# Cross-attention of a decoder: keys placed by DMA, scores from high and low parts, another order of the loop

## What is computed

```python
def _L0_xattn_ref(q, k, v, Wq, bq, Wk, bk, Wv, bv, Wo, bo):
    HEADS, D_MODEL = 16, 256
    D_K = D_MODEL // HEADS
    qh = (q @ Wq + bq).reshape(B, LQ, HEADS, D_K).transpose(0, 2, 1, 3)
    kh = (k @ Wk + bk).reshape(B, LKV, HEADS, D_K).transpose(0, 2, 1, 3)
    vh = (v @ Wv + bv).reshape(B, LKV, HEADS, D_K).transpose(0, 2, 1, 3)
    scores = jnp.einsum('bhqd,bhkd->bhqk', qh, kh) * (1.0 / np.sqrt(D_K))
    out = jnp.einsum('bhqk,bhkd->bhqd', jax.nn.softmax(scores, axis=-1), vh)
    return out.transpose(0, 2, 1, 3).reshape(B, LQ, D_MODEL) @ Wo + bo

x = x + _L0_attn_ref(_layernorm(x), ...)
x = x + _L0_xattn_ref(_layernorm(x), ctx_512, ctx_512, ...)
x = x + _L0_ffn_ref(_layernorm(x), ...)
```

## Time and profile before

| | us |
|---|---|
| median of 3 runs | 3157.49 (3156.26 to 3159.41) |
| the profiled execution | 3159.65 |
| its span, from the first instruction to the last | 3158.1 |
| of it PE busy | 2933.1 (93%) |
| DVE busy | 2325.5 (74%) |
| ACT busy | 1862.7 (59%) |
| POOL busy | 921.5 (29%) |

### The profile page before, as it was taken

How to read it: one execution, slowest core, us unless ns; L and a number is a source line. 1 busy time by engine, 2 the same in 40 slices (tenths; PEclk the granted TensorE clock), 3 DMA queues, 4 the chain that set the end, 5 groups by cost and what they waited for, 6 DMA issues and landing times. The chain is left out here.

```text
span 3158.1 us, 35422 instructions
## 1 busy us (share of the span) xinstructions
PE 2933.1 (93%) x11342; PEld 1989.8 (63%) x11343; DVE 2325.5 (74%) x3334; ACT 1862.7 (59%) x2796; POOL 921.5 (29%) x590
## 2 busy tenths in 40 slices
PE   4799999999999999999999999999999977997995
PEld 3566666666666665666566656665666635775563
DVE  7778888888887888887878788879787826763111
ACT  3666676667666776777677767776777713441121
POOL 5004231423152315231513151315131133333002
PEclk8899999999999999999999999999999987996998
DMA  5001101110111001100110011001100008000012
GB/s 129 1 1 23 26 8 32 27 27 6 30 27 27 12 25 27 27 17 19 26 27 17 19 26 27 17 19 26 28 17 4 1 3 269 0 0 24 12 45 77
DMA packets 210193, 92.90 MB, mean 29 GB/s; under 512 B 147056, under 2 KB 203632, under 8 KB 210000
## 3 DMA queue, kind: packets, MB, share of 16 engines
q1 hardware_dynamic: 207360, 83.30, 10.2%
q0 software_dynamic: 2640, 7.21, 0.7%
HBM read 80.24 MB, written 10.22 MB: 29 GB/s over the span
## 5 line engine op out<-in xcount | busy, mean ns | idle before, releaser
L341 PE MATMUL PS<-XTHI,WHI 128*128 128x512 f32 x1536 | 655.5, 427 | 60.8 <-DVE EX L641 41.5
L342 PE MATMUL PS<-XTLO,WHI 128*128 128x512 f32 x1536 | 614.1, 400 | 0.0
L343 PE MATMUL PS<-XTHI,WLO 128*128 128x512 f32 x1536 | 613.6, 399 | 0.0
L269 POOL TENSOR_TENSOR RSTD<-MV,EPS 128x4 f32<-128x4 f32 x68 | 41.1, 605 | 1537.7 <-DVE MV L713 1529.8
L391 PE MATMUL Y<-H,W2S 128*128 128x512 f32 x1024 | 458.2, 596 | 2.7 <-DVE R L703 2.7
L391 PE MATMUL Y<-ATT,WO 128*128 128x512 f32 x1024 | 451.7, 594 | 4.1 <-ACT ATT L540 2.7
L540 ACT ACTIVATE ATT<-INV,CC,CE 128x128 f32<-128x128 f32 x1024 | 424.9, 481 | 3.7 <-DVE INV L687 3.7
L341 PEld LDWEIGHTS PS<-XTHI,WHI 128*128 128x128 f32 x1536 | 294.5, 192 | 153.6 <-issue 64.6
L505 ACT ACTIVATE EX<-PS,BNEG 128x512 f32<-128x512 f32 x256 | 169.8, 686 | 309.9 <-PE PS L343 307.6
L342 PEld LDWEIGHTS PS<-XTLO,WHI 128*128 128x128 f32 x1536 | 294.8, 192 | 83.6 <-issue 20.3
L343 PEld LDWEIGHTS PS<-XTHI,WLO 128*128 128x128 f32 x1536 | 294.0, 191 | 70.0
(11 more groups left out here) (180 smaller groups left out, 4823.9 us busy)
## 6 DMA issues: line engine op xcount, KB each, us to landing
STAGE<-L_attn_Wk SPq DMA_DIRECT2D x128, 64.0 KB, 2.1
STAGE<-L_attn_Wv SPq DMA_DIRECT2D x128, 64.0 KB, 2.1
STAGE<-L_attn_Wq SPq DMA_DIRECT2D x128, 64.0 KB, 2.1
WO<-L_attn_Wo SPq DMA_DIRECT2D x8, 1024.0 KB, 5.5
W2S<-L_attn_W SPq DMA_DIRECT2D x8, 1024.0 KB, 5.6
STAGE<-L_attn_W SPq DMA_DIRECT2D x64, 128.0 KB, 3.7
WGU<-L_ffn_r_gate SPq DMA_DIRECT2D x8, 512.0 KB, 10.2
WGU<-L_ffn_r_up SPq DMA_DIRECT2D x8, 512.0 KB, 9.5
```

Of the source, the lines that this page charges most:

```text
L341: nc.tensor.matmul(out, whi[:, kc, :], xhi[:, kc, :], start=(kc == 0), stop=False)
L342: nc.tensor.matmul(out, whi[:, kc, :], xlo[:, kc, :], start=False, stop=False)
L343: ins = nc.tensor.matmul(out, wlo[:, kc, :], xhi[:, kc, :], start=False, stop=(kc == KD - 1))
```

## The change

The host hands the context over transposed, and it is loaded per sequence straight into CT; CTXS, CSEQ, their copies and one transpose go. ScalarE writes the keys and the queries as high parts (KT[:, 0], QHI) in the type float32r; a new step `residues` on VectorE computes their low parts from the same PSUM bank (KT[:, 1], QLO). KX is filled with zeros once, by GpSimd, and `apart` is now on SyncE: eight DMAs for each half and sequence, each of which copies both parts of the keys of one head, 16 partitions by 2 by 128, to that head's columns. MASK and the mask product go. `scores` sums three float32r products in place of one float32 product. KT has one buffer: `qk(b+1)` waits until the DMAs of sequence b have landed. The loads for the experts move from SyncE's queue to GpSimd's. And the order changes: on TensorE make_qk(b+1) goes to the head of the iteration, and scores(b+1, 0) behind project(b-1) and turn_inputs(b+2); on ScalarE qk(b+1) goes ahead of turned_weights(b, 0); on VectorE residues(b+1) stands ahead of shifted(b, 1).

```diff
-        QT = sb("XQT", [P, 2, KD, P])
-        KT = sb("XKT", [P, 2, KD, P])
-        KX = sb("XKX", [P, 2, CH, SEQ])
+        QHI = sb("XQHI", [P, 2, KD, P], F32R)
+        QLO = sb("XQLO", [P, 2, KD, P], F32R)
+        KT = sb("XKT", [P, 2, KD, P], F32R)
+        KX = sb("XKX", [P, KD, 2, CH, SEQ], F32R)
...
+            def apart(i, j, c):
+                b = 2 * i + j
+                sp.wait_ge(k_lo, b + 1)
+                if not (type(i) is int and b == 0):
+                    sp.wait_ge(s_mm, b * KD + c - 1)
+                for h in range(CH):
+                    rows = slice(h * XK, (h + 1) * XK)
+                    sp.dma_start(KX[rows, c, :, h, :].bitcast(F32), KT[rows, :, c, :].bitcast(F32)).then_inc(kx[c], 16)
...
-                sp.dma_start(CTXS[:, bs, :], ctx_in[bs, :, :].rearrange("b s d -> s b d")).then_inc(x_in[k], 16)
+            def load_ctx(i, j):
+                b = 2 * i + j
+                if not (type(i) is int and i == 0):
+                    sp.wait_ge(v_mm, b - 1)
+                sp.dma_start(CT[:, j, :], ctx_in[bass.ds(b, 1), :, :].rearrange("b d s -> d (b s)")).then_inc(ct_in[j], 16)
...
+            sp.wait_ge(kx_zero, 1)
+            def sequence(i, j, more):
+                for c in range(KD):
+                    apart(i, j, c)
+                if more:
+                    load_ctx(i + 1, j)
...
+            nc.gpsimd.memset(KX[:, :, :, :, :].bitcast(F32), 0.0).then_inc(kx_zero, 1)
...
-            def apart(i, j, c):
-                u = (2 * i + j) * KD + c
-                pool.wait_ge(kt, 2 * i + (j + 1))
-                if not (type(i) is int and u < 2):
-                    pool.wait_ge(s_mm, u - 1)
-                nc.gpsimd.tensor_tensor(KX[:, c, :, :], bcast(KT[:, j, c, :], CH), MASK[:, :, :], ALU.mult).then_inc(kx, 1)
...
-                nc.tensor.transpose(A[:, 2 * P:3 * P], CSEQ[:, j, :], ident[:, :]).then_inc(zct_mm, 1)
...
+            def make_qk(b, j, i):
+                pe.wait_ge(ct_in[j], 16 * i + 16)
                 pe.wait_ge(zct, b + 1)
...
             def make_v(b, j):
-                pe.wait_ge(qt, b + 1)
-                pe.wait_ge(kt, b + 1)
+                pe.wait_ge(q_lo, b + 1)
...
             def scores(b, j, c):
                 u = b * KD + c
-                pe.wait_ge(kx, u + 1)
+                pe.wait_ge(kx[c], (b + 1) * 16 * CH)
+                pe.wait_ge(q_lo, b + 1)
                 if not (type(b) is int and u < 2):
                     pe.wait_ge(sh, u - 1)
                 for hf in range(2):
-                    ins = nc.tensor.matmul(S[:, c, hf * 512:(hf + 1) * 512], QT[:, j, c, :],
-                                           KX[:, c, hf * 4:(hf + 1) * 4, :].rearrange("p h s -> p (h s)"),
-                                           start=True, stop=True)
+                    out = S[:, c, hf * 512:(hf + 1) * 512]
+                    hi, lo = (KX[:, c, part, hf * 4:(hf + 1) * 4, :].rearrange("p h s -> p (h s)") for part in range(2))
+                    nc.tensor.matmul(out, QHI[:, j, c, :], hi, start=True, stop=False)
+                    nc.tensor.matmul(out, QHI[:, j, c, :], lo, start=False, stop=False)
+                    ins = nc.tensor.matmul(out, QLO[:, j, c, :], hi, start=False, stop=True)
                 ins.then_inc(s_mm, 1)
...
             def run(i, j):
                 b, before, after, after2 = step(i, j)
                 k = 1 - j
+                if after:
+                    make_qk(b + 1, k, i + j)
                 scores(b, j, 1)
                 turn_weights(b, j, 0)
-                if after:
-                    make_qk(b + 1, k)
                 weigh(b, j, 0)
                 if after:
                     make_v(b + 1, k)
                 turn_weights(b, j, 1)
                 if before:
                     turn_output(b - 1, k, b * KD + 1)
-                if after:
-                    scores(b + 1, k, 0)
                 if before:
                     project(b - 1, k)
                 if after2:
                     turn_inputs(b + 2, j)
+                if after:
+                    scores(b + 1, k, 0)
                 if before:
                     pe.wait_ge(upd, b)
                 weigh(b, j, 1)
...
             def qk(b, j):
                 act.wait_ge(qk_mm, b + 1)
+                if not (type(b) is int and b == 0):
+                    for c in range(KD):
+                        act.wait_ge(kx[c], b * 16 * CH)
                 for c in range(KD):
-                    ins = nc.scalar.activation(KT[:, j, c, :], A[:, (2 + c) * P:(3 + c) * P], ACT.Identity,
+                    ins = nc.scalar.activation(KT[:, 0, c, :], A[:, (2 + c) * P:(3 + c) * P], ACT.Identity,
                                                bias=BK[:, c:c + 1])
                 ins.then_inc(kt, 1)
                 for c in range(KD):
-                    ins = nc.scalar.activation(QT[:, j, c, :], A[:, c * P:(c + 1) * P], ACT.Identity, bias=BQ[:, c:c + 1])
+                    ins = nc.scalar.activation(QHI[:, j, c, :], A[:, c * P:(c + 1) * P], ACT.Identity, bias=BQ[:, c:c + 1])
                 ins.then_inc(qt, 1)
...
-                turned_weights(b, 0)
                 if after:
                     qk(b + 1, k)
+                turned_weights(b, 0)
                 weights(b, 1)
...
-                nc.vector.tensor_copy(CSEQ[:, j, :], CTXS[:, b, :])
...
+            def residues(b, j):
+                dve.wait_ge(qt, b + 1)
+                for c in range(KD):
+                    ins = nc.vector.scalar_tensor_tensor(KT[:, 1, c, :], A[:, (2 + c) * P:(3 + c) * P], BK[:, c:c + 1],
+                                                         KT[:, 0, c, :].bitcast(F32), ALU.add, ALU.subtract)
+                ins.then_inc(k_lo, 1)
+                for c in range(KD):
+                    ins = nc.vector.scalar_tensor_tensor(QLO[:, j, c, :], A[:, c * P:(c + 1) * P], BQ[:, c:c + 1],
+                                                         QHI[:, j, c, :].bitcast(F32), ALU.add, ALU.subtract)
+                ins.then_inc(q_lo, 1)
...
+                if after:
+                    residues(b + 1, k)
                 shifted(b, 1)
                 output(b, j, 0)
...
+    arrays["ctx_512"] = np.ascontiguousarray(np.swapaxes(arrays["ctx_512"], 1, 2))
```

More of the change, by code:

```diff
@@ L860, in cross_attention @@
         BOX = sb("XBO", [P, D])
-        MASK = sb("XMASK", [P, CH, SEQ])
         HALF = sb("XHALF", [P, SEQS])
@@ L886, in cross_attention @@
         x_in = [sem(f"xx_in{k}") for k in range(2)]
+        ct_in = [sem(f"xct_in{j}") for j in range(2)]
         w_in, bias_in = (sem(n) for n in ("xw_in", "xbias_in"))
-        set0, ones_set, v0, r0, mask_set, kx = (sem(n) for n in ("xset0", "xones_set", "xv0", "xr0", "xmask_set", "xkx"))
+        set0, ones_set, v0, r0, kx_zero = (sem(n) for n in ("xset0", "xones_set", "xv0", "xr0", "xkx_zero"))
+        kx = [sem(f"xkx{c}") for c in range(KD)]
+        k_lo, q_lo = sem("xk_lo"), sem("xq_lo")
         prep, z, mx, sh, rd, o, v1, ob, upd = (
@@ L912, in _ @@
             sp.dma_start(BOX[:, :], bo.unsqueeze(0).to_broadcast([P, D])).then_inc(bias_in, 16)
[L914 to L926, removed]
-                    sp.dma_start(ffn.WGU[:, e, m, :, :], rows(a["L0_ffn_r_" + n][e, :, :])).then_inc(ffn.routed_in, 16)
-                sp.dma_start(ffn.WD[:, e, :, :], rows(a["L0_ffn_r_down"][e, :, :])).then_inc(ffn.routed_in, 16)
+            sp.wait_ge(kx_zero, 1)
[4 more added lines that the diff above has]
+                    load_ctx(i + 1, j)
+            for j in range(2):
+                sequence(0, j, True)
+            with sp.Fori(1, SEQS // 2 - 1, 1) as i:
+                for j in range(2):
+                    sequence(i, j, True)
+            for j in range(2):
+                sequence(SEQS // 2 - 1, j, False)
         @block.gpsimd
@@ L952, in _, with rows @@
             rstd(0)
[L953 to L970 removed]
+            rstd(1)
+            def rows(w):
+                return w.rearrange("(c p) n -> p c n", p=P)
+            pool.dma_start(ffn.GT[:, :, :], rows(a["L0_ffn_gate_w"]), allow_slow_non_contiguous=True
+                         ).then_inc(ffn.shared_in, 16)
+            for m, n in enumerate(("gate", "up")):
+                pool.dma_start(ffn.SGU[:, m, :, :], rows(a["L0_ffn_shared_" + n])).then_inc(ffn.shared_in, 16)
+            pool.dma_start(ffn.SD[:, :, :], rows(a["L0_ffn_shared_down"])).then_inc(ffn.shared_in, 16)
+            pool.wait_ge(ffn.zero_set, 1)
+            pool.dma_start(ffn.rows_in[:, :].rearrange("(u p) d -> p u d", p=P), bcast(ffn.ZERO[:, :], RT)
+                         ).then_inc(ffn.zeroed, 16)
+            for e in range(a["L0_ffn_r_gate"].shape[0]):
+                for m, n in enumerate(("gate", "up")):
+                    pool.dma_start(ffn.WGU[:, e, m, :, :], rows(a["L0_ffn_r_" + n][e, :, :])).then_inc(ffn.routed_in, 16)
+                pool.dma_start(ffn.WD[:, e, :, :], rows(a["L0_ffn_r_down"][e, :, :])).then_inc(ffn.routed_in, 16)
```

(7 more changed lines are left out.)

24 lines of the change are left out of this document (5 added, 19 removed).

## The result

The changed kernel takes **3287.4 us** (median of 4 runs, 3285.9 to 3288.9) against 3158.2 before (4 runs, 3156.3 to 3159.4): ratio 1.0411, 95% interval 1.0395 to 1.0428, some 129 us slower. The profiled executions differ by 128.9 us (3287.0 against 3158.1).

The account below looks back on a forecast made before the run. TensorE was taken to bound the old kernel; the new loop is one chain. Iterations 110, start 2.7 and contention 5 sum to +118 on 3159.65, 3277.3; the median 2.2 lower, 3275 us, range 3215 to 3322.

Parts of the forecast that it names:

- part 4: Cross-attention order: the new loop becomes one chain through the engines, 16.6 us an iteration at full clock.
- part 6: TensorE's clock in the cross-attention: at 1.2 GHz a little over half the time, making 21.5 us an iteration.
- Rival (b): Clock stays at 1.2 GHz in the cross-attention: 25 us an iteration, +167, 3324 us; chance 0.09.
- part 5: SyncE's key and context DMAs: free in steady state, +2.7 us at the start, 5 us for contention with expert weights.
- rival (c): Key DMAs bound, landing as for weights: 22 in place of 5, 3292 us; chance 0.10 together with rival (e).
- The start: Beginning of the cross-attention: the first key DMAs replace one mask product by 5.3 us, +2.7 us.
- the contention: Key DMAs landing later while 16 MB of expert weights load from GpSimd's queue: 5 us taken, between 0 and 22.
- parts 1 and 3: Scores: six float32r products take 1.39 us against 1.80; VectorE's four residues add 1.1 us an iteration.
- rival (e): Score products take 0.45 us as in float32, parts save nothing: 18 us, 3293; chance 0.10 together with rival (c).
- part 2: GpSimd's mask products go; VectorE's normalisation gets 2.05 us shorter, worth nothing since VectorE waits for the projection anyway.

Follow-up runs that it names:

- the filled kernel: Changed kernel with 20 extra float32 products of 120 columns on TensorE in each iteration, where TensorE waits anyway: 3237.1 us.
- late loads: Changed kernel with one wait added, so GpSimd starts loading the expert weights only after twelve score groups: 3280.4 us.
- no transfers: Changed kernel without the 16 key transfers of each iteration, the separated keys staying zero: 3269.4 us.
- context alone: Kernel before with only the host-transposed context, without TensorE's third transpose and ScalarE's second copy: 3159.9 us, 0.9997.
- context with fillers: The context alone kernel with three extra float32 products of 120 columns in each iteration, ahead of TensorE's wait for updated rows: 3151.3 us.

## Why the prediction was right

It said 3275, slower with 0.94; 3287 came out, by the mechanism forecast. Step by step:

- **The chain (part 4): right as a chain.** 16.6 us at the full clock; the traced iteration gives 16.6 after make_qk's share of the slow clock, the filled kernel 16.4 to 17.1. But "this decides" was half the truth. The order is one of two loops of that length, and undoing it gives nothing while the transfers stay. What decides is that neither loop fits into 12.5 us.
- **The clock (part 6): right, in kind and size.** 21.5 forecast, 21.16 measured, of which 4.1 are the clock (forecast 4.9). Granted clock 0.73 against "near 0.7". Rival (b) fell. A mean of 0.73 is 1.2 GHz for 54% of the time; the forecast's 58% stood between two worked ends and was not itself worked out, so that it lay so near is partly luck. The trace has the clock at 1.00 from 2860.80 to 2863.00, with turned weights in it, and the ten iterations average 0.73. The rule for transposes cited in the prediction from the Trainium skill (TensorE: Matmul & The Clock Gate, section Part 4: PE-mode transpose) would have held the loop at 1.2 GHz and given 3324; the trace does not bear that out for this mix, in which transposes alternate with products, and the kernel before, with 21 of them an iteration, already ran at 0.94.
- **The transfers (part 5): free in the steady stretch, right; sizes off.** An issue lasts 0.59 us, not 0.42, and sixteen take 10.2 us, not 7.2, so SyncE's queue issues for 10.2 of 21.2 us; the landing is 1.8, not 2.1. The issue's price had been taken from a transfer of another shape (64 KB from HBM); these are 16 KB between SBUF partitions. At 0.64 from issue to issue it stayed under the 0.8 from which rival (c) decides.
- **The start: the term that was too small.** Forecast 2.7 for the first transfers and 5 for the contention. Measured: 9.5 us up to the first addition of BOX (39.37 against 29.85 from the first load) and 9.4 in the interval behind it (21.41 against 12.02), 18.9 in all. The two runs that take something away split it: 11.9 us are the load beside the transfers (late loads), within the 0 to 22 that were given, but not near the 5 taken; 4.0 more are the transfers undisturbed (late loads against no transfers), against 2.7; the last 3.0 are in neither term and stay when the transfers are gone. Landing rose to 8.4 us and an issue to 1.66 at most, as this row has it:

```profile
L908 SPq DMA_DIRECT2D XKX<-XKT x256: 585/592/1663, 2628.5 to 2955.6; - x128
...
DMA to landing us min/median/max: 1.8/1.8/8.4
```

  The Trainium skill (DMA: Bandwidth & Descriptors, section Queues, rings and completion order) has each DMA engine take turns between queues packet by packet, by which this term was to be near 0. No run here shows how the engines take turns; the measurement decides on what was drawn from it: the term is 11.9, not 0, and the issues themselves get slower too.
- **Product and residue (parts 1 and 3): right.** Products 0.23 us apart at the full clock, 0.43 at half of it, so rival (e) fell; the residues take 1.1 us an iteration as forecast (2862.07 to 2863.19), of which 0.7 shows in the time behind the start.
- **The mask product (part 2): right.** The normalisation takes 0.41 us instead of 2.46, and nothing comes of it: VectorE then waits 3.10 us for the projection all the same (at 2870.50).
- **The sum.** Forecast 110 + 7.7 = 118. Measured: the 14 further intervals take 21.15 us each against 13.58, 106; the start 18.9, the later beginning 1.8, the stage's end and the experts 2.2: 129. The 12 us by which 3275 fell short are the start, 11 more than forecast; the later beginning and the stage's end, 4 us that no term had, are made up for by the iterations, 4 less than forecast. The range as stated, up to 3322, left out rival (b)'s own figure of 3324, of which it was to take most.

## What to carry to other kernels

In a loop over engines, count loops and not steps: walk each way round (through the order, through each transfer, through GpSimd) and take the longest. When an edit is undone and nothing comes back, undo it together with the next suspect; here the two gave 1 and 18 us singly and 118 together. A transfer's issue is to be priced by one of its own shape, and its landing by what else is loading. Where TensorE waits in a chain that has slack, cheap products into PSUM columns whose content is used up can pay for themselves by the clock; first look whether the chain can be cut, which gave more.

## What the hardware showed that was not expected

- A DMA of 16 partitions from SBUF to SBUF (2 x 128 values for each) holds SyncE's queue for 0.59 us, 0.64 from issue to issue, and lands in 1.8 us. Beside a bulk load on GpSimd's queue the first 16 took 13.9 us to issue and 5.5 to land (median), with the load moved away 11.1 and 1.8. The bulk pieces of 512 KB landed in 23.5 us, against 10.2 from SyncE's queue before; GpSimd issued them about 0.8 us apart and SyncE mostly over 1, and what the queue itself does to the landing is not separated.
- Three float32 products of 120 columns an iteration, ahead of one wait, took the clock from 0.94 to 1.00 and the iteration from 13.50 to 12.78 us, with 20 transposes in each iteration (context alone against context with fillers).
